# Layer 0 of a graph network: TensorE's semaphores raised by a drain behind each group of products, instead of by the last product

## The reference

```
q = feat @ Wq.T + bq;  k = feat @ Wk.T + bk;  v = feat @ Wv.T + bv        # feat: layer norm of x
e = einsum('ehd,ehd->eh', q[src], k[dst]) * scale                         # 4 heads of 64
sa = exp(e - segment_max(e, dst)[dst]) / segment_sum(...)[dst]            # softmax by destination
rst = segment_sum(sa * v[src], dst)
skip = feat @ Wskip.T + bskip;  rst = g * skip + (1 - g) * rst            # g: a sigmoid gate
x = x + prelu(layernorm(rst))
```

## Time and profile before

| | |
|---|---|
| median of 3 runs | 7408.09 us |
| the profiled execution | 7403.44 us, span 7401.6 us |
| busy in the span | PE 4849.9 us (66%), DVE 4162.4 (56%), ACT 2632.7 (36%), POOL 3349.8 (45%) |
| mean granted TensorE clock | 0.785 of full speed |
| projection | 602 to 1159 us |
| edges | 1159 to 2630 us |
| finish and hop projection | 2630 to 3124 us |

### The profile page before, as it was taken

How to read it: one execution, slowest core, us unless ns; L and a number is a source line. 1 busy time by engine, 2 the same in 40 slices (tenths; PEclk the granted TensorE clock), 3 DMA queues, 4 the chain that set the end, 5 groups by cost and what they waited for, 6 DMA issues and landing times. The chain is left out here.

```text
span 7401.6 us, 90008 instructions
## 1 busy us (share of the span) xinstructions
PE 4849.9 (66%) x23010; PEld 3528.7 (48%) x23011; DVE 4162.4 (56%) x9337; ACT 2632.7 (36%) x4979; POOL 3349.8 (45%) x3352
## 2 busy tenths in 40 slices
PE   1794345777777787258787631435556555999999
PEld 1783123555555577235555421323444443566656
DVE  5882124999998976222222386856666666444443
ACT  0231002555555532024333332145555553222222
POOL 1005744777777767456666432156666663000000
PEclk6776677899898855578898855667777777999999
DMA  2000126888888876133332201755555554000000
GB/s 78 0 0 21 51 75 216 246 247 245 246 247 244 244 186 159 30 109 88 79 80 75 73 3 44 238 169 149 149 151 150 149 151 136 15 15 15 15 15 10
DMA packets 618649, 853.64 MB, mean 115 GB/s; under 512 B 209780, under 2 KB 421723, under 8 KB 618013
## 3 DMA queue, kind: packets, MB, share of 16 engines
q0 software_dynamic: 159136, 383.90, 20.1%
q1 hardware_dynamic: 325037, 418.50, 17.6%
q10 hardware_dynamic: 134372, 50.10, 2.8%
HBM read 694.03 MB, written 164.92 MB: 116 GB/s over the span
## 5 line engine op out<-in xcount | busy, mean ns | idle before, releaser
L1027 POOL DMA_INDIRECT b_got<-tmp_l_table,b_src x928 | 1011.4, 1090 | 414.6 <-issue 263.5
L2214 POOL DMA_INDIRECT w_got<-tmp_l_table,w_src x928 | 889.7, 959 | 490.3 <-issue 256.8
L2934 POOL DMA_INDIRECT t_got<-tmp_f_table,t_src x672 | 635.9, 946 | 410.8 <-DVE t_sums L3012 205.9
L2463 PE MATMUL w_pa<-w_got,w_hot 128*128 128x264 f32 x1856 | 661.2, 516 | 180.1 <-issue 89.0
L1273 PE MATMUL b_pk<-b_keys,b_hot_t 128*128 x1856 | 558.7, 454 | 289.3 <-issue 177.0
L2463 PEld LDWEIGHTS w_pa<-w_got,w_hot 128*128 128x128 f32 x1856 | 449.0, 255 | 301.2 <-issue 200.4
L1273 PEld LDWEIGHTS b_pk<-b_keys,b_hot_t 128*128 128x128 f32 x1856 | 396.1, 224 | 380.6 <-issue 318.3
L3422 DVE SCALAR_TENSOR_TENSOR l_accs<-l_po,l_prob,l_accs 128x256 f32 (+1 forms) x392 | 173.5, 480 | 597.3 <-PE l_po L3528 597.3
L3473 ACT ACTIVATE l_h<-l_ph,l_bn 128x896 f32<-128x896 f32 x224 | 245.1, 1097 | 661.0 <-PE l_ph L3518 661.0
L1288 PE MATMUL b_pa<-b_got,b_hot 128*128 128x260 f32 x1856 | 469.2, 398 | 6.2 <-DVE b_acc L1200 2.2
L3056 PE MATMUL t_po<-t_w,t_hid 128*128 128x256 f32 x1568 | 407.4, 410 | 91.4 <-issue 71.8
(11 more groups left out here) (564 smaller groups left out, 10153.2 us busy)
## 6 DMA issues: line engine op xcount, KB each, us to landing
tmp_g_acc<-b_acc SPq DMA_DIRECT2D x232, 260.0 KB
w_spread<-tmp_g_rel_rows SPq DMA_DIRECT2D x232, 256.0 KB
t_spread<-tmp_f_rel_rows SPq DMA_DIRECT2D x170, 256.0 KB
b_spread<-tmp_g_rel_rows SPq DMA_DIRECT2D x116, 256.0 KB
e_attr<-in_edge_attr ACTq DMA_DIRECT2D x103, 256.0 KB
tmp_f_experts<-t_y SPq DMA_DIRECT2D x28, 896.0 KB
y_y<-tmp_f_experts SPq DMA_DIRECT2D x28, 896.0 KB, 10.9
b_got<-tmp_l_table,b_src POOLq DMA_INDIRECT x928
```

What stands on the lines that cost most here:

```text
L1027: pool.indirect_dma_start(out=got[:, m % NB, u, :], out_offset=None, in_=T["l0_table"], in_offset=bass.IndirectOffsetOnAxis(ap=src[:, m * ...
L2214: pool.indirect_dma_start(out=got[:, p % 3, u, :], out_offset=None, in_=T["l1_table"], in_offset=bass.IndirectOffsetOnAxis(ap=src[:, p * R ...
L2463: mm = pe.matmul(pa[:, (k * RS + n) % SUMS, 0:WV], hot[:, (k * B4 + b) % 3, u - b * U, :], got[:, k, u, 0:WV], start=(u == 2 * n), stop=(u ...
L2934: pool.indirect_dma_start(out=got[:, g % DEPTH, u, :], out_offset=None, in_=T["f_table"], in_offset=bass.IndirectOffsetOnAxis(ap=src[:, g ...
```

## The change

Wherever PE raised a semaphore with the last product of a group, in the three stages, an instruction `pe.drain()` now follows the group and raises it. `Norm.tensor` is shared with other stages and has an argument for it, which the projection alone sets. The products, their order and all waits stay.

```diff
-    def tensor(self, pe, K, c):
+    def tensor(self, pe, K, c, drain=False):
...
-        ins.then_inc(self.turned, 1)
+        if drain:
+            pe.drain().then_inc(self.turned, 1)
+        else:
+            ins.then_inc(self.turned, 1)
...
-                    ins.then_inc(projected, 1)
-
-            n.tensor(pe, K, 0)
+                    pe.drain().then_inc(projected, 1)
+
+            n.tensor(pe, K, 0, True)
...
-                    n.tensor(pe, K, c + 1)
+                    n.tensor(pe, K, c + 1, True)
...
-                mm.then_inc(expanded, 1)
+                pe.drain().then_inc(expanded, 1)
...
-                    mm.then_inc(summed, 1)
+                    pe.drain().then_inc(summed, 1)
...
-                pe.transpose(p_one, one[:, at % LOOP, :], K["ident"][:, :]).then_inc(one_turned, 1)
+                pe.transpose(p_one, one[:, at % LOOP, :], K["ident"][:, :])
+                pe.drain().then_inc(one_turned, 1)
...
-                pe.matmul(p_chain, of_head[:, :], ends[:, :, :].rearrange("p r k -> p (r k)"), start=True, stop=True).then_inc(chained, 1)
+                pe.matmul(p_chain, of_head[:, :], ends[:, :, :].rearrange("p r k -> p (r k)"), start=True, stop=True)
+                pe.drain().then_inc(chained, 1)
...
-                    mm.then_inc(h_turned, 1)
+                    pe.drain().then_inc(h_turned, 1)
...
-                mm.then_inc(projected, 1)
+                pe.drain().then_inc(projected, 1)
```

More of the change, by code:

```diff
@@ L1294, in turn_scores @@
                     pe.wait_ge(weights_ready, p)
-                pe.transpose(p_one, one[:, at % LOOP, :], K["ident"][:, :]).then_inc(one_turned, 1)
+                pe.transpose(p_one, one[:, at % LOOP, :], K["ident"][:, :])
+                pe.drain().then_inc(one_turned, 1)
             def chain_ends(p):
                 pe.wait_ge(ends_ready, p + 1)
-                pe.matmul(p_chain, of_head[:, :], ends[:, :, :].rearrange("p r k -> p (r k)"), start=True, stop=True).then_inc(chained, 1)
+                pe.matmul(p_chain, of_head[:, :], ends[:, :, :].rearrange("p r k -> p (r k)"), start=True, stop=True)
+                pe.drain().then_inc(chained, 1)
             def spread_tops(p):
                 pe.wait_ge(tops_ready, p + 1)
-                pe.matmul(p_tops, to_head[:, :], c_top[:, 1:1 + 2 * R], start=True, stop=True).then_inc(tops_out, 1)
+                pe.matmul(p_tops, to_head[:, :], c_top[:, 1:1 + 2 * R], start=True, stop=True)
+                pe.drain().then_inc(tops_out, 1)
             def turn_weights(p):
@@ L1308, in turn_weights @@
                     pe.wait_ge(rhs_ready, B4 * p)
-                pe.matmul(p_fade, first_hot[:, :], fade_mat[:, :], start=True, stop=True).then_inc(fade_out, 1)
+                pe.matmul(p_fade, first_hot[:, :], fade_mat[:, :], start=True, stop=True)
+                pe.drain().then_inc(fade_out, 1)
                 pe.wait_ge(exp_ready, p + 1)
-                pe.transpose(p_weight, exps[:, :], K["ident"][:, :]).then_inc(weights_out, 1)
+                pe.transpose(p_weight, exps[:, :], K["ident"][:, :])
+                pe.drain().then_inc(weights_out, 1)
             def round_(p, at, two_ahead, ahead, now_, behind):
```

## The result

The change makes the kernel slower: 7771.87 us (median of 4 runs, 7745.80 to 7785.65) against 7393.69 us of the kernel before on the same chip (4 runs, 7355.66 to 7427.44). The ratio is 1.051, 95% interval 1.045 to 1.057. The forecast of 7355 us was wrong, and its range, 7195 to 7460, missed too. The nearest case was the held drains at 7660 us, to which I gave a chance of 0.21.

The account below looks back on a forecast made before the run. Raises held late beside POOL's indirect DMAs bound the projection and finish, DVE's chain the edges. 7403.4 - 121 (projection) - 55 (hop) + 125 (edges) = 7352 for the profiled execution, 7355 us as median; range 7195 to 7460.

Parts of the forecast that it names:

- the held drains: Rival, all stages: drains wait for late product completion; no gain in projection and hop, edges +252, 7660 us; chance 0.21.
- within 0.1 us of the product's end: All three stages: a drain raises its semaphore this soon after the last product; 0.05 us was taken.
- -121: Projection: prompt raises make POOL's scatter the stage's end, hiding the drains; 121 us saved.
- -55: Finish and hop projection: prompt raises let the stage end with POOL, hiding 14 drains; 55 us saved.
- the rule: Trainium skill's advice against the change: attach the increment to the matmul; a drain waits until the engine is fully idle.
- The edges' 26.2 us a round: Edges: PE's summed round with 17 drains, against 24.05 now, giving +125 us over 58 rounds.
- the restarts: Edges, PE after each drain: 0.35 us before an expansion, 0.42 before a batch's first sum, 0.15 before a second.
- 1.99 us: Edges: the round's first expansion at the upper clock level, instead of 3.62 us at 1.2 GHz.
- 2.41: Edges: us from the turn's drain to the first expansion, 1.94 of it the load of tile numbers.
- the slow-clock rival: Edges: first expansion stays at 1.2 GHz, round 27.8 us, +219 us, total 7451 us; chance 0.13.
- PE takes over from DVE: Edges: PE's 26.2 us round becomes the bound, DVE's own 23.4 us of work fitting beside it.
- The missing gain: Projection and hop projection: the forecast savings of 121 and 55 us from prompt raises.

Follow-up runs that it names:

- three kernels without: Kernel before plus edge drains behind expansions alone, behind sums alone, or all with an earlier tile-number load; projection and hop unchanged: 7630.21, 7708.56, 7804.54 us.
- the load out: Kernel before plus all edge drains, loop reusing round 2's tile numbers: 6800.30 us against 6793.60 on a chip without holds, 7443.59 against 7406.19 with holds.
- the scatter alone: Kernel before, but POOL starts its scatter only when all 49 projection tiles are done; on a chip with holds the stage took 679.5 us.
- the gathers left out: Kernel before plus all edge drains, POOL gathering only the first 12 batches: round 27.76 us on a chip without holds, 27.65 with holds.

## Why the prediction was wrong

**The raise "within 0.1 us of the product's end": false beside POOL's indirect DMAs.** This step carried -121 and -55. The row behind it was a drain at a stage's end, with POOL long finished, and I took it for one in the middle of POOL's work. The product's shown end isn't its completion there, if completion is what a drain waits for. What the drain waits for comes late, on chips of one kind, as the increment did. In the projection that gave +16 instead of -121, because the drain also keeps PE from the second tile of a hold; on C the stage takes 571 us with the drains and 558 to 564 in three kernels without. In the hop projection nothing was gained: the 11 us of A are within what the stage varies on C with no change in it (474 to 490 us in three kernels), and the changed kernel takes 504 there. The Trainium skill has both halves: "PSUM — Partial Sum Buffer", section "Engine vs sequencer instructions", says that updates fire on completion and that a drain waits for the engine to be idle, and "Perfetto Trace Analysis", section "Tensor Engine Instruction (MATMUL, LD_WEIGHTS)", that the end of a product is estimated and its semaphore update comes once PSUM has acknowledged the writes. The trace agrees as far as it goes: on A up to 35 us lay between a product's shown end and its drain's end. That it is PSUM's acknowledgement which comes late, no run shows. I set the rule aside in the prediction for a 32.7 us that fits it.

**The edges' 26.2 us a round: the restarts were right, three terms were not.** On chip B, without holds, PE's round is 28.12 us. The first expansion, which I took at 1.99 us, has a median of 3.49 there: 1.50 more. I chose the upper clock level because the expansion at 1818.36 had it after 1.44 us idle; this one comes after 3.19. It was at the lower level in nearly every round of the kernel before too (median 3.56 us on A), where PE had the time for it; the forecast counted on the drains to lift it. The stretch from the turn's drain to that expansion, taken as 2.41, is 3.19: 0.78 more, since the load of tile numbers takes 2.57 us instead of 1.94 and starts only when the array is empty. 26.2 + 1.5 + 0.8 = 28.5, so by this difference the 17 restarts themselves were if anything 0.4 us too dear in all. That is the slow-clock rival (27.8), which I gave 0.13. The third term is the hold, absent on B and about 1.4 us a round on A: 28.1 + 1.4 = 29.5 of the 30.07 measured; the last 0.5 us are not accounted for.

**"PE takes over from DVE": right**, as DVE's waits on B show, in the edges of before (1200 to 2400 us) and with the drains (1200 to 2600 us):

```profile
DVE b_acc L1200 <- PE b_pa L1288: 38.6, 100, 0.6
```
```profile
DVE b_acc L1200 <- PEq L1289: 269.5, 148, 4.0
```

What my sum hid is how near the edge it was: with the load out, PE's chain with all 17 drains fits into a round of 23.64 us.

**The held-drains rival** had the mechanism and the sign, and its no gain in the projection and the hop. Its place in the edges was wrong: it had the first expansion held for 2.2 us a round; in the trace of after, from 1234 to 2900 us, one of 60 expansions at 1.2 GHz is held, by 0.2 us, but 49 of 160 at 2.4 GHz are, 45 of them as the fourth of their round.

**The missing gain** could not have shown on either kind of chip seen here: on those with holds the drain waits too, and on those without there is nothing to win.

## What to carry to other kernels

A drain behind a group makes everything that the sequencer did under the array's cover bare. Here the restarts, most of them 0.2 to 0.4 us, fitted into the time that PE had over; what cost was the longest sequencer work behind a drain, a load of registers (2.6 us), and the clock level of the expansion after it (1.2 GHz). Take a semaphore that is late by the profile's ends for a late completion until the opposite is shown. Here moving its increment did not help, and taking away what delays it (POOL's stream of indirect DMAs, by pauses tied to the waiting engine's progress) did. Run such a change on more than one chip before explaining it.

## What the runs showed of the hardware

- Chips differ. Beside POOL's indirect DMAs drains end after their product by up to 35 us on A, 47 on C, 17 on E and 3.4 on F (there in the edges alone); on B and D no added one by more than 0.023 us. The kernel before takes 7394 to 7444 us on the first kind and 6794 to 6797 on the second, the same kind in every run on a chip (7 each on C and E, 13 on D). With POOL idle the projection runs alike on both. That the holds are the whole of the difference is not shown: some 390 of the 605 us between A and B (7401.6 and 6796.9) lie behind the three stages, where no experiment looked. What causes them, and whether it is in the chip itself or around it, isn't known.
- Not PE's completions alone are unlike. From 640 to 1000 us, beside the projection, the trace of before on A has 578 increments by the scatter's DMAs, where the 255 DMAs issued then bring 16 each; on B it has 4062 for 254 (in the kernel with the hop's drains alone). With the scatter alone on E (900 to 1260 us) it is 4108 for 258 again. Whether the increments come bundled or the trace misses them isn't known.
- The Trainium skill, "SBUF — State Buffer", section "Who interferes with whom", says of the ports of SBUF that PE never waits on anyone. No run shows that a port holds PE here; but the sentence can't be carried over to what follows a product on the first kind of chip: 21 of 25 drains in the projection of the changed kernel are held beside POOL's scatter, and none after it.
- The load of eight registers takes 1.94 us (median) on PE's sequencer in the kernel before and with drains behind the expansions alone, 2.54 with drains behind the sums alone, 2.57 with all, 2.29 with all and the gathers left out. What it waits for is open.
- In the rounds shown the clock was at 1.2 GHz after 3.66 us idle, a turn of 0.47 us and 0.42 us idle ahead of the expansion, and stayed at 2.4 GHz after 0.23 us idle, a turn of 0.30 and 0.32 idle.
